# When a graph kernel's gathers may start: after an expansion, or after the landing of the block's rows of B

## What is computed

```python
msg_in = concatenate([x[src], x[dst]])            # 256 per edge
h = relu(msg_in @ Wm1 + bm1)
h = relu(h @ Wm2 + bm2)
messages = h @ Wm3 + bm3
agg = segment_sum(messages, dst) / max(count, 1)
upd = relu(concatenate([x, agg]) @ Wn1 + bn1) @ Wn2 + bn2
out = layernorm(x + (x + upd))
```

## Time and profile before

| | |
|---|---|
| three runs | 1202.29 us (1199.84 to 1202.59) |
| span of the profiled execution | 1416.6 us |
| the profiled execution's own time, apart from its span | not given |
| PE, PEld busy | 88%, 83% of the span |
| DVE, ACT, POOL busy | 69%, 52%, 56% |
| DMA engines, mean busy over the main loop | 51% |

### The profile page before, as it was taken

One profiled execution on the slowest core, in us unless ns is written; L12 is line 12 of the kernel. 1 busy time (PEld: TensorE's weight loads), 2 busy tenths in 40 slices (PEclk: granted clock), 3 DMA queues, 4 the chain that ended last, 5 costly groups with the idle time before them and its releaser, 6 DMA issues.

```text
span 1416.6 us, 33766 instructions
## 1 busy us (share of the span) xinstructions
PE 1249.7 (88%) x9614; PEld 1172.0 (83%) x9615; DVE 979.6 (69%) x2072; ACT 740.6 (52%) x1392; POOL 786.5 (56%) x814
## 2 busy tenths in 40 slices
PE   6978888888888888888888889988999989899997
PEld 6868888888888888888888888888888888888886
DVE  6846666766766666766766766767767767777676
ACT  3544555555555555555555555555554555545585
POOL 2166666666666666666666666666666666564000
PEclk9999999999999999999999999999999999999999
DMA  9665555545545555555545555455545454554022
GB/s 308 274 234 156 146 144 151 149 141 151 151 140 150 152 142 147 151 143 147 152 139 150 146 143 151 145 144 152 139 147 151 138 150 144 145 151 142 10 67 86
DMA packets 135605, 211.42 MB, mean 149 GB/s; under 512 B 24247, under 2 KB 102669, under 8 KB 134030
## 3 DMA queue, kind: packets, MB, share of 16 engines
q1 hardware_dynamic: 98030, 108.43, 25.3%
q0 software_dynamic: 37536, 102.55, 25.1%
HBM read 188.09 MB, written 22.80 MB: 149 GB/s over the span
## 4 chain that ended last, share of the span: by engine, by line
PE 80%; issue 12%; DVE 2%; SPq 1%; another core or an unknown queue 1%; DMA 1%; ACT 1%; DVEq 1%; ACTq 0%
PE bank L1437 39%; PE bank L1413 11%; PE bank L1324 6%; PE sums L1345 4%; PE sums L1341 4%; PE sums L1347 3%; PE sums L1349 3%; PE bank L1478 2%; PE sums L1491 1%; PE bank L1234 1%; PE bank L1219 1%; PE bank L1461 1%; PE sums L1219 1%; DMA b_win<-b_table 1%
## 5 line engine op out<-in xcount | busy, mean ns | idle before, releaser
L630 POOL DMA_INDIRECT a_edge<-a_table,src_idx x782 | 767.1, 981 | 457.8 <-remote 268.2
L1437 PE MATMUL bank<-w,h 128*128 128x256 f32 x4692 | 661.4, 283 | 104.9 <-issue 102.1
L1437 PEld LDWEIGHTS bank<-w,h 128*128 128x128 f32 x4692 | 596.5, 188 | 119.7 <-issue 118.7
L1106 DVE SCALAR_TENSOR_TENSOR h<-bank,h 128x512 fp32r<-128x512 f32 x391 | 268.7, 687 | 338.4 <-issue 326.7
L732 ACT ACTIVATE h<-bank 128x512 fp32r<-128x512 f32 x391 | 233.8, 598 | 475.3 <-remote 439.2
L721 ACT COPY bank<-b_bc 128x512 f32<-128x512 f32 x391 | 231.5, 592 | 115.2 <-issue 66.7
L1118 DVE SCALAR_TENSOR_TENSOR h_lo<-bank,h_hi 128x512 fp32r<-128x512 f32 x391 | 266.5, 681 | 0.1
L1413 PE MATMUL bank<-ident,a_edge 128*128 128x128 f32 x1564 | 237.4, 274 | 21.1 <-issue 16.6
L740 ACT ACTIVATE h_hi<-bank 128x512 fp32r<-128x512 f32 x391 | 232.6, 595 | 2.8 <-PE bank L1437 2.8
L1413 PEld LDWEIGHTS bank<-ident,a_edge 128*128 128x128 f32 x1564 | 180.3, 140 | 40.5 <-issue 34.2
L1324 PE MATMUL bank<-onehot_t,b_win 128*128 128x256 f32 x782 | 190.3, 325 | 0.0
(11 more groups left out here) (190 smaller groups left out, 682.7 us busy)
## 6 DMA issues: line engine op xcount, KB each, us to landing
b_win<-b_table SPq DMA_DIRECT2D x391, 128.0 KB
rel<-rel_dram SPq DMA_DIRECT2D x196, 128.0 KB
a_edge<-a_table,src_idx POOLq DMA_INDIRECT x782
a_table<-work SPq DMA_DIRECT2D x12, 512.0 KB, 4.6
b_table<-work SPq DMA_DIRECT2D x5, 1024.0 KB
b_table<-h SPq DMA_DIRECT2D x4, 1024.0 KB
f_x<-in_x SPq DMA_DIRECT2D x12, 256.0 KB, 5.2
b_table<-a_edge SPq DMA_DIRECT2D x3, 1024.0 KB, 5.8
```

Source lines behind the costliest of these rows:

```text
L630: pool.indirect_dma_start(a_edge[:, b % R * TB + t, :], None, a_table, bass.IndirectOffsetOnAxis(ap=src_idx[:, b * TB + t:b * TB + t + 1], ...
L1106: dve.scalar_tensor_tensor(h1[:, k % U, 1, :], bank[k % 2][:, :], 0.0, h1[:, k % U, 0, :].bitcast(F32), ALU.max, ALU.subtract).then_inc(s_ ...
L1437: ins = pe.matmul(to, h1[:, j, a, h * EB + t * P:h * EB + (t + 1) * P], w2[:, b, h, :], start=False, stop=(a == 1 and h == KH - 1), skip_g ...
```

## The change

The wait at line 628 goes over to the landing of the block's `b_win` (the load is itself issued after an expansion that frees the buffers). SyncE's body is reordered: for each pair of blocks k, k + 1 it waits for the expansion of k - 4, loads `b_win` of k, waits for that of k - 3, and loads `rel` of the pair and `b_win` of k + 1. In the first body, where there is nothing to wait for, the order stays `rel`, `b_win`, `b_win`.

```diff
             def body(i):
                 first = load_words(sp, words_sp, i * U, U, PAD_DST)
-                for k in range(U):
-                    if there(i, k - RB):
-                        sp.wait_ge(s_ex, i * U + (k - RB + (2 if k % 2 == 0 else 1)))
-                    if k % 2 == 0:
-                        sp.dma_start(rel[:, k // 2, :].rearrange("p (b e) -> p b e", b=2),
-                                     rel_dram[bass.ds(i * U + k, 2), :].partition_broadcast(P)
-                                     ).then_inc(s_rc[k // 2], 16)
+                def load_rows(k):
                     if there(i, k):
                         sp.dma_start(b_win[:, k % RB, :].bitcast(F32),
                                      b_table[bass.ds(first[k] * 2, P), :]).then_inc(s_bw[k % RB], 16)
+
+                for k in range(0, U, 2):
+                    if there(i, k - RB):
+                        sp.wait_ge(s_ex, i * U + (k - RB + 1))
+                        load_rows(k)
+                        sp.wait_ge(s_ex, i * U + (k - RB + 2))
+                    sp.dma_start(rel[:, k // 2, :].rearrange("p (b e) -> p b e", b=2),
+                                 rel_dram[bass.ds(i * U + k, 2), :].partition_broadcast(P)
+                                 ).then_inc(s_rc[k // 2], 16)
+                    if not there(i, k - RB):
+                        load_rows(k)
+                    load_rows(k + 1)
             bodies(sp, body)
...
             for b in range(NBE):
                 if b >= R:
-                    pool.wait_ge(s_ex, b - R + 1)
+                    pool.wait_ge(s_bw[b % RB], b // RB * 16 + 16)
                 for t in range(TB):
                     pool.indirect_dma_start(a_edge[:, b % R * TB + t, :], None, a_table,
```

## The result

| | before | changed |
|---|---|---|
| runs, median | 1201.1 us (4 runs) | 1306.8 us (4 runs, 1303.2 to 1308.8) |
| ratio, 95% interval | | 1.0869 (1.0853 to 1.0886) |
| profiled execution: time, span | 1202.8, 1201.0 (a second profile, below) | 1308.2, 1306.5 |
| main loop, us a block | 2.57 | 2.84 |

The account below looks back on a forecast made before the run. PE's train of 2.58 us a block was taken to bound the kernel. Terms 0 - 0.3 + 1 + 0.5, about +1.2 us on 1202.3, gave 1203.5 us, range 1198.5 to 1228.

Parts of the forecast that it names:

- What bounds the kernel: Main loop: PE's train of 2.58 us a block sets the timed runs; the profile's extra 212 us are pauses from profiling.
- Work and SyncE's order: Same loads, gathers and bytes, 0; SyncE's reordered loads 0, except a gain of 0.3 us at the end, at most 1.
- The new wait: Gathers waiting for B: loop from expansion b - 4 to b takes 9.7 us, within four blocks' 10.32, 0.6 to spare.
- same: Likeliest case: the cover over the new wait holds, with a range of 1200 to 1206 us; chance 0.48.
- Who queues behind the wait: On POOL only later gathers; on DVE `onehot_t` about 2 us later, with the shift not growing: 0.
- Start: First blocks: POOL loses 2.4 us once from block 4's gather on; cost 0 to 2.4 us, taken as 1.
- Tails: Main loop: late transfers now and then eat the 0.6 us of cover; estimated at 0.5 us.
- The first: Slower rival: the main loop's wait chain exceeds four blocks; +37 us to 1239, +135 at the upper end; chance 0.33.
- The late view: Slower rival: every second expansion is seen 2 us late in timed runs too; +82 us, 1284; chance 0.06.
- The faster one: Rival: earlier even-block loads and less crowded gathers remove small hidden data stalls in the loop; -5 us, 1197; chance 0.13.
- GpSimd as the bound: Rival: later gathers stretch by 0.05 us, two make 2.66 us a block; +31 us; chance within the first slower rival's 0.33.
- Signs: Profile marks: POOL waits name `b_win`, DVE waits for `a_edge`, PE's `onehot_t` waits under 20, transposes' span near 1218 us.

Follow-up runs that it names:

- second profile: The kernel before, unchanged, profiled again: time 1202.8 us, span 1201.0 us.
- order alone: SyncE's new load order kept from the changed kernel, gathers waiting for the expansion four back as before: 1201.6 us, ratio 0.9989.
- `rel` last: The changed kernel with `rel` issued behind the odd block's load of B instead of ahead of it: 1219.6 us, ratio 1.0132.
- the new wait alone: The kernel before with only the gathers' wait for the landing of `b_win`, SyncE's order as before: 1596.3 us, ratio 1.3271.

## Why the prediction was wrong

*What bounds the kernel* held. PE's train of 2.58 us times 390, with 198 around it, is the timed kernel; the second profile shows it. That the pauses come with the profile was half right: with one profiled execution.

*Work and SyncE's order* held: order alone 1201.6, expected 0 with a gain of at most 1.

*The new wait* is the step that failed, by the size of its sum, 9.7 us for a loop that measured 11.16, not by its mechanism: "the loop from expansion b - 4 back to expansion b" is what sets the time. Term by term against the turn above:

| term | predicted | measured |
|---|---|---|
| expansion to B's issue | 0.74 | 0.68 |
| L, B's landing | 3.1 | 3.35 |
| GpSimd's reaction | 0.1 | 0.26 |
| first gather and gap | 1.28 | 1.44 |
| G, the second gather's landing | 3.1 | 3.98 |
| mask and both sides | 0.6 | 0.53 |
| PE | 0.88 | 0.92 |
| sum | 9.8 | 11.16 |

The prediction's 9.7 counts the 0.1 beside the mask once, though it says "on both sides". 0.9 of the missing 1.4 us is G: 3.1 predicted, 3.98 measured. I took the middle between 2.0, below which no landing was possible by the rows, and 4.12 for both; for L that was near, for G it was the upper end that held. The lower end came from a gather that ran after a quiet time, which the loop never has, so the nearest row was the busy one. The rule that the text set, "It decides from L + G = 6.8", was right: it was 7.33. By its price, 98 us for every us over the span, the turn gives (11.16 - 10.32) x 98 = 82 us. Over the whole trace, 11.0 against 10.3 for four blocks, the loop is worth some 66 us after the twelfth block; the rest of the 106 comes with the ends of ranges, for which the sum had no term, and with the first blocks.

So a cover of 0.6 us between bounds 4.2 us apart (7.5 to 11.7) was no reason for "same" at 0.48: most of the sum's span above 9.7 lay over 10.32. The range, too, reached only to a loop of 10.6 us (1228), less than half way to an upper end that was itself only a row, and the 11.16 lies beyond it.

*Who queues behind the wait* held as far as VectorE's shift goes: ACT's bias copy now waits for `h_lo` at almost every block (458.5 us in 385 waits), and no wait of PE for it is on the page. Its 0 did not hold for PE: with masks just in time, a block in which a range ends takes 3.44 us against 2.71 for the others. The prediction has no word on these blocks.

*Start*, 1 us, can't be judged well. The first transpose, at 89.3, comes ahead of the term. The first twelve blocks took 37.1 us against 30.8, of which the steady loss explains some 3; but with SyncE's order alone, a kernel without loss, its one profile has 34.2. *Tails*, 0.5 us, were too small: where the loop closes, 11 to 17 us stay, with `rel` last 13 of them at the ends of ranges.

*The rivals.* The first came true. The late view was refuted by the second profile. The faster one was refuted by the order alone. GpSimd as the bound was refuted by leaving out an eighth of its gathers. The Trainium skill's page "DMA: Bandwidth & Descriptors" (Anatomy of one DMA, on the path that GpSimd issues) puts a transfer at about 2.0 us and its bytes at 436 GB/s; 2.3 us for 128 KB, an estimate by it, would have made the loop 8.1. This case's trace doesn't agree: the chain has 3.35 and 3.98 for 128 KB each, the latter with some 0.95 of the gather's issue in it. The measurement decides.

*Signs.* POOL waits for `b_win`, as said, and the gather's mean stayed (974 ns); but PE and its loader wait for `onehot_t` 176 times, where the text wanted fewer than 20 and named hundreds as wrong. The first to last transpose, said to stay near 1218 us, fell to 1108, since the first profile's pauses are gone.

## What to carry to other kernels

A wait that looks covered has to be priced as a closed loop: from the release of a buffer, through every transfer and reaction, back to the next release, against the blocks that the ring of buffers spans. Putting one landing behind another adds a whole latency, with its issue and the reaction to it, to that loop (here 0.68 + 3.35 + 0.26 us), and each us over the span is paid at 1 / depth in every block. When the bounds of the latencies put the loop on both sides of the span, say so in the chances; and if a profiled execution is much longer than the runs, take its waits with care; its lengths of single instructions held here (a gather 0.981 us, 0.965 in the second profile). A wait that comes just in time also takes away the slack that hid other work of the engine: look for blocks that differ from the rest, here those in which a range ends.

## What the runs showed of the hardware

- With other transfers in flight, at a mean DMA share of 0.57, 128 KB took 3.57 us in the median (3.09 to 3.98) from SyncE's issue to the landing in the changed kernel's chain, and a gather of 128 rows of 1 KB 3.92 us (3.42 to 5.47) from its start on GpSimd. One 128 KB transfer issued directly ahead of the load cost the changed kernel 87 us through its loop.
- GpSimd starts a gather 0.26 us after a landing and also 0.26 us after an expansion; a landing has no dearer wait. Back to back, the gap is 0.30.
- One profiled execution of the kernel before was 214 us longer than its runs, with a pause of PE in every second block; the next one, of the same kernel, had none.
- TensorE's granted clock stayed at 1.00 (2.4 GHz) from 120 us on in the changed kernel, where PE's longest wait for a mask after 95 us was 3.1 us and half of the blocks took less than 2.65 us. With the new wait alone, 3.58 us a block, it fell to 0.50 (1.2 GHz) 34 times; twelve matmuls took 2.53 in place of 1.57 us.
